# Causal attention beside a mixture of experts: heads divided by VectorE and projected by pairs, and the combine spread over more units

## The reference

```python
xn  = layernorm(x)                        # no gamma, no beta
# attention: 16 heads of 64, RMS norm with gamma, causal softmax
normed = xn / max(norm(xn), 1e-12) * 128 ** 0.5 * gamma
q, k, v = split(normed @ w_qkv)           # 128 x 3072
attn = softmax(where(causal, q @ k.T / 8, -max))
attention = (attn @ v, heads side by side) @ w_out      # 1024 x 128
# experts: top 2 of 8, 128 -> 512 -> 128, relu
experts = layernorm(xn + sum over the two of weight * expert(xn)) * ffn_gamma + ffn_beta
out = x + attention + experts
```

## Time and profile before

| | |
|---|---|
| median of 3 runs | 1457.95 us (1456.97 to 1460.27) |
| profiled execution, its own time | 1463.13 us |
| its span (first to last instruction) | 1461.4 us |
| mean granted TensorE clock | 0.958 |
| TensorE busy | 1351.4 us, 92% |
| VectorE busy | 1038.1 us, 71% |
| ScalarE busy | 947.8 us, 65% |
| GpSimd busy | 867.2 us, 59% |

### The profile page before, as it was taken

The page is one execution under the profiler, slowest core; times in us unless marked ns, Lnnn a source line. Parts: engine busy times, 40 slices in busy tenths (PEclk is TensorE's granted clock), DMA queues, the critical chain, the costliest instruction groups (busy, mean ns, idle before and its releaser), DMA issues.

```text
span 1461.4 us, 27770 instructions
## 1 busy us (share of the span) xinstructions
PE 1351.4 (92%) x8360; PEld 1124.9 (77%) x8361; DVE 1038.1 (71%) x2674; ACT 947.8 (65%) x2094; POOL 867.2 (59%) x1304
## 2 busy tenths in 40 slices
PE   4569998999879999999999899899899999899998
PEld 4446666999757888788788788788788788788886
DVE  5656654222257788888888888888888888888773
ACT  2435544555447677677777677677677777677775
POOL 3426651332227568667667667767766766766666
PEclk9669999999869999999999999999999999999999
DMA  6222221222122022112112212112212212211112
GB/s 204 89 60 63 63 54 55 77 75 77 47 57 52 3 41 50 29 30 51 35 33 44 43 30 46 38 36 42 41 30 46 42 32 39 48 30 32 30 30 59
DMA packets 131078, 72.47 MB, mean 50 GB/s; under 512 B 80216, under 2 KB 116864, under 8 KB 130944
## 3 DMA queue, kind: packets, MB, share of 16 engines
q1 hardware_dynamic: 114304, 54.18, 18.2%
q0 software_dynamic: 4096, 8.40, 1.9%
q10 hardware_dynamic: 12544, 8.29, 1.9%
HBM read 20.47 MB, written 16.52 MB: 25 GB/s over the span
## 4 chain that ended last, share of the span: by engine, by line
PE 53%; DVE 11%; issue 5%; ACT 2%; DMA 1%; SPq 0%; DVEq 0%; POOLq 0%; ACTq 0%
PE max_ps L1281 8%; PE score_ps L1299 6%; PE score_ps L1298 6%; PE misc_ps L1341 6%; PE head_ps L1318 5%; PE head_ps L1327 5%; PE head_ps L1325 5%; PE head_ps L1323 5%; DVE max_ps L1140 4%; PE misc_ps L1262 3%; DVE x_row L1156 2%; PE misc_ps L1256 2%; DVE q_a L1126 1%; PE misc_ps L1257 1%; PE misc_ps L1258 1%
## 5 line engine op out<-in xcount | busy, mean ns | idle before, releaser
L1032 POOL TENSOR_TENSOR p_lo<-probs,p_hi 128x512 fp32r<-128x512 f32 (+3 forms) x560 | 536.1, 958 | 188.5 <-ACT p_hi L1084 183.9
L1082 ACT ACTIVATE probs<-score_ps 128x512 f32<-128x512 f32 (+3 forms) x768 | 377.5, 492 | 257.0 <-PE score_ps L1299 243.8
L1140 DVE CUSTOM_DVE_ANT_0 max_ps<-max_ps,mask 128x128 f32<-128x128 f32 (+7 forms) x512 | 390.7, 763 | 111.1 <-PE max_ps L1281 87.8
L1298 PE MATMUL score_ps<-q_a,k_a 128*128 128x512 f32 (+3 forms) x768 | 304.3, 396 | 0.2 <-ACT p_hi L1084 0.2
L1281 PE MATMUL max_ps<-k_a,q_a 128*128 128x512 f32 (+3 forms) x768 | 238.6, 366 | 54.2 <-DVE shift L1140 45.0
L1024 POOL TENSOR_SCALAR_AFFINE_SELECT probs<-probs 128x128 f32<-128x128 f32 x512 | 153.7, 300 | 202.3 <-ACT p_hi L1084 136.9
L1299 PE MATMUL score_ps<-q_b,k_b 65*128 65x512 f32 (+3 forms) x768 | 269.6, 351 | 0.0
L1084 ACT ACTIVATE p_hi<-score_ps 128x512 fp32r<-128x512 f32 (+3 forms) x560 | 263.1, 470 | 0.0
L1318 PE MATMUL head_ps<-probs,v_all 128*65 128x128 f32 (+3 forms) x1088 | 248.7, 310 | 0.0
L1281 PEld LDWEIGHTS max_ps<-k_a,q_a 128*128 128x128 f32 x768 | 140.8, 195 | 114.9 <-DVE shift L1140 86.5
L1323 PE MATMUL head_ps<-p_hi,v_hi 128*65 128x512 f32 (+3 forms) x560 | 210.3, 376 | 0.0
(11 more groups left out here) (165 smaller groups left out, 2086.6 us busy)
## 6 DMA issues: line engine op xcount, KB each, us to landing
k_a<-k_a SPq DMA_DIRECT2D x64, 256.0 KB
q_b<-q_a SPq DMA_DIRECT2D x64, 256.0 KB
q_b<-shift SPq DMA_DIRECT2D x512, 0.5 KB
sorted_x<-zeros SPq DMA_DIRECT2D x13, 384.0 KB, 5.0
rows<-sorted_x SPq DMA_DIRECT2D x39, 128.0 KB, 2.1
sorted_y<-result ACTq DMA_DIRECT2D x39, 128.0 KB, 1.8
acc<-in_L_attn_x_dram SPq DMA_DIRECT2D x4, 512.0 KB, 7.2
x_row<-in_L_attn_x_dram SPq DMA_DIRECT2D x8, 256.0 KB
```

Source lines behind the costliest of these rows:

```text
L1032: pool.tensor_tensor(p_lo[:, lo_slot(g, c), w0:w1], probs[:, slot, w0:w1], p_hi[:, slot, w0:w1].bitcast(F32), ALU.subtract).then_inc(pool_ ...
L1082: ins = act.activation(probs[:, slot, 0:width], src[:, 0:width], ACT.Exp, scale=SCALE)
L1140: dve.tensor_tensor_reduce(out=max_ps[:, at:at + width], in0=max_ps[:, at:at + width], in1=mask[:, SEQ - width:SEQ], scale=-1.0, scalar=-M ...
L1298: pe.matmul(dst, k_a[i][s][:, keys], q_a[i][s][:, qs], start=True, stop=False)
```

## The change

- **Projection by pairs.** For all heads but the last two of each stage, ScalarE copies the head with its row of sums into raw. SP moves the 1024 sums out of their one partition into [128, 8] (sums, chunk 5 of the next unit), VectorE inverts them (chunk 8), SP writes them to a row in DRAM (inverse, chunk 10) and reads the row back into 64 partitions (spread, chunk 0 of the unit after). At chunks 3 and 4 of that unit VectorE multiplies the two halves of the head with it into stacked, rows 0 to 63 for the even head, 64 to 127 for the odd one. At chunks 7 and 9 of an odd unit TensorE projects both heads at once with 128 rows, in two pieces of four tiles, and VectorE adds each piece to acc in one instruction. The last two heads of each stage go the old way.
- **Combine.** 33 steps a group instead of 45, seven to a unit at chunks 0, 2, 4, 5, 7, 9 and 11, in units 3 to 7 of the group. Centring goes to ScalarE (chunks 7 to 10 of unit 2). The norm and gamma are one step, the scale and the addition to acc another; ffn_beta is added to acc by GpSimd, in 8 instructions at the start of the expert stage, before it waits for w1_split.
- **nT in DRAM.** nT is stored to DRAM in the routing stage in 8 DMAs, and ScalarE's queue loads 1024 tokens of it for each batch's projection of v (tokens). The new tiles take its room.
- **Start and end.** The pieces of q and k come in the order q, k, q, k, and SP copies each half by itself (eight DMAs of half the size). Only t0 to t3 of the first unit's maxima stand before its first score, t4 to t7 at its chunks 0 and 1, and those of the second unit from chunk 2. The last batch is stored in three DMAs, of 3, 3 and 2 tiles.

```diff
+                        pool.wait_ge(beta_loaded, 16)
+                        for g in range(ALL_TILES // GROUP):
+                            some = acc[:, g * GROUP:(g + 1) * GROUP]
+                            pool.tensor_tensor(some, some, fbeta[:].unsqueeze(1).broadcast_to([P, GROUP, D]),
+                                               ALU.add).then_inc(beta_added, 1)
...
+                    return own + [(W + 1, t) for t, at in enumerate(SECOND_MAX_AT) if at == c]
+                return [(W + 1, t) for t, at in enumerate(MAX_AT) if at == c and W + 1 < WL]
 
             PROJECT_AT = [{0: 0, 1: 1, 3: 2, 5: 3}, {1: 4, 5: 5}]
 
             STARTS = [6 * k for k in range(ALL_TILES // GROUP)]
             GATHER_AT = [(1, 8)] + [(1, c) for c in (9, 10, 11)] + [(2, c) for c in (1, 3, 5, 7, 9)]
             SCATTER_AT = [(g, c) for g in range(7) for c in range(10)][:2 * ALL_TILES]
-            COMBINE = ([("center", q) for q in range(GROUP)]
-                       + [("first", q) for q in range(GROUP)] + [("second", q) for q in range(GROUP)]
+            COMBINE = ([("first", q) for q in range(GROUP)] + [("second", q) for q in range(GROUP)]
                        + [("stats", q) for q in range(GROUP)] + [("aggr", 0), ("var", 0)]
                        + [("rsqrt", n) for n in range(RSQRT_STEPS)]
-                       + [(kind, q) for kind in ("norm", "gamma") for q in range(GROUP)]
-                       + [(kind, q) for q in range(GROUP) for kind in ("beta", "add")])
+                       + [(kind, q) for q in range(GROUP) for kind in ("gamma", "add")])
             COMBINE_STEPS = len(COMBINE)
-            COMBINE_AT = [(2, c) for c in (2, 4, 5, 6)]
-            COMBINE_AT += [(g, c) for g in (3, 5) for c in (0, 0, 1, 2, 3, 4, 5, 5, 6, 7, 8, 9, 11, 11)]
-            COMBINE_AT += [(7, c) for c in (0, 0, 1, 2, 3, 3, 3, 4, 4, 5, 5, 7, 7)]
+            COMBINE_AT = [(g, c) for g in (3, 4, 5, 6) for c in (0, 2, 4, 5, 7, 9, 11)]
+            COMBINE_AT += [(7, c) for c in (0, 2, 4, 5, 7)]
+            CENTRE_AT = [(2, c) for c in (7, 8, 9, 10)]
             assert len(COMBINE_AT) == COMBINE_STEPS
-            Y_AT = [7, 9, 11]
...
+            Y_AT = {7: 0, 9: 1}
+            LAST_Y_AT = {8: 0, 10: 1, 11: 2}
...
+                    if W % 2 and c in Y_AT and stacks(W - 2):
+                        order += [(kind, W // 2 - 1, Y_AT[c]) for kind in ("y", "add")]
+                    if W == WL - 1 and c in LAST_Y_AT:
+                        order += [(kind, W - 1, LAST_Y_AT[c]) for kind in ("last_y", "last_add")]
+                    if c:
+                        order += [("shift", *item) for item in max_items(W, c - 1)]
+                    if stacks(W - 1):
+                        order += [(kind, W - 1, 0) for kind, at in (("sums", 5), ("invert", 8), ("inverse", 10))
+                                  if at == c]
+                    if stacks(W - 2):
+                        order += [(kind, W - 2, n) for kind, n, at in (("spread", 0, 0), ("norm", 0, 3),
+                                                                      ("norm", 1, 4)) if at == c]
...
+                        if (unit - start, c) in CENTRE_AT:
+                            order.append(("centre", CENTRE_AT.index((unit - start, c)), k))
+                        order += [("combine", n, k) for n, at_ in enumerate(COMBINE_AT) if at_ == (unit - start, c)]
...
+                        if kind == "sums":
+
+                            W = g
+                            sp.wait_ge(heads_out[0], W + 2)
+                            sp.wait_ge(heads_out[1], W + 2)
+                            sp.dma_start(sums[:, W % 2], raw[HEAD:HEAD + 1, W % 2]).then_inc(sums_moved[W % 2], 16)
+                        if kind == "inverse":
+                            W = g
+                            sp.wait_ge(sums_inverted, n_stacked(W) + 1)
+                            sp.dma_start(inverse_row[W % 2].rearrange("(p j) -> p j", p=P), inverse[:, W % 2]
+                                         ).then_inc(inverse_moved[W % 2], 16)
+                        if kind == "spread":
+                            W = g
+                            sp.wait_ge(inverse_moved[W % 2], n_spread(W) * 16)
+                            if native and W == W0:
+                                for q in range(BATCH):
+                                    sp.wait_ge(nT_stored[q], 16 * SEQ // BANK)
+                            if W > W0:
+                                sp.wait_ge(norm_done, 2 * n_stacked(W - 1) + 2)
+                            sp.dma_start(rden_all[:], inverse_row[W % 2].partition_broadcast(HEAD)
+                                         ).then_inc(spread[W % 2], 16)
...
+                    def load_tokens(Q):
+                        cols = slice(Q % BATCH * SEQ, (Q % BATCH + 1) * SEQ)
+                        if Q > Q0:
+                            act.wait_ge(misc_ready, place[("project", Q - 1, 5)] + 1)
+                        if Q < BATCH:
+                            act.wait_ge(nT_stored[Q], 16 * SEQ // BANK)
+                        act.dma_start(tokens[:], nT_dram[:, cols]).then_inc(tokens_loaded, 16)
...
+                        elif kind == "centre":
+                            row, t = x_row[:, g], c * GROUP + g
+                            act.wait_ge(x_again, c * 16 + 16)
+                            act.activation(row, row, ACT.Identity, scale=rstd[:, t:t + 1],
+                                           bias=centre_bias[:, t:t + 1]).then_inc(centred, 1)
...
+                            if half == 0 and W - W0 >= 2:
+                                act.wait_ge(norm_done, 2 * n_stacked(W - 2) + 2)
...
-                        elif kind == "norm":
-                            ins = dve.tensor_scalar(row, row, gmom[:, n, 0:1], gvar[:, 1, n:n + 1],
-                                                    ALU.subtract, ALU.mult)
                         elif kind == "gamma":
-                            ins = dve.tensor_tensor(row, row, fgamma[:], ALU.mult)
-                        elif kind == "beta":
-                            ins = dve.tensor_tensor(row, row, fbeta[:], ALU.add)
+                            if step == COMBINE.index(("gamma", 0)):
+                                dve.wait_ge(small2_loaded, 16)
+                            ins = dve.scalar_tensor_tensor(out=row, in0=row, scalar=gmom[:, n, 0:1], in1=fgamma[:],
+                                                           op0=ALU.subtract, op1=ALU.mult)
                         elif kind == "add":
-                            ins = dve.tensor_tensor(acc[:, t], acc[:, t], row, ALU.add)
+                            ins = dve.scalar_tensor_tensor(out=acc[:, t], in0=row, scalar=gvar[:, 1, n:n + 1],
+                                                           in1=acc[:, t], op0=ALU.mult, op1=ALU.add)
                         ins.then_inc(comb_step, 1)
...
+                    def invert(W):
+                        dve.wait_ge(sums_moved[W % 2], n_spread(W) * 16)
+                        if W - W0 >= 2:
+                            dve.wait_ge(inverse_moved[W % 2], n_spread(W - 2) * 16)
+                        dve.reciprocal(inverse[:, W % 2], sums[:, W % 2]).then_inc(sums_inverted, 1)
+
+                    def normalise(W, half):
+
+                        s, cols = W % 2, slice(half * BANK, (half + 1) * BANK)
+                        rows = slice(s * HEAD, (s + 1) * HEAD)
+                        if half == 0:
+                            dve.wait_ge(spread[s], n_spread(W) * 16)
+                            if s == 0 and W // 2 > Q0:
+                                dve.wait_ge(misc_ready, place[("y", W // 2 - 1, 1)] + 1)
+                        dve.tensor_tensor(stacked[rows, cols], raw[0:HEAD, s, cols], rden_all[:, cols],
+                                          ALU.mult).then_inc(norm_done, 1)
+
+                    def after_combine(n):
+                        if n:
+                            dve.wait_ge(comb_step, n)
+
+                    def add_y(Q, n):
+                        u = place[("y", Q, n)]
+                        rows = acc[:, Q % BATCH * TILES + n * GROUP:Q % BATCH * TILES + (n + 1) * GROUP]
+                        dve.wait_ge(misc_ready, u + 1)
+                        dve.tensor_tensor(rows, misc_ps[u % 2][:].rearrange("p (t d) -> p t d", d=D), rows,
+                                          ALU.add).then_inc(y_added, 1)
+
...
+                    def project_pair(Q, n):
+                        dst = misc_bank("y", Q, n)
+                        pe.wait_ge(norm_done, 2 * n_stacked(2 * Q + 1) + n + 1)
+                        if n == 0:
+                            pe.wait_ge(wout_loaded, Q // BATCH * 16 + 16)
+                        for q in range(GROUP):
+                            q0 = (n * GROUP + q) * P
+                            ins = pe.matmul(dst[:, q * D:(q + 1) * D], stacked[:, q0:q0 + P], wo[:],
```

(3 more changed lines are left out.)

652 lines of the change are left out of this document (329 added, 323 removed).

## The result

The changed kernel takes 1490.16 us (median of 5 runs, 1486.9 to 1490.5), beside 1459.35 of the kernel before on the same chip: ratio 1.0206, 95% interval 1.019 to 1.0222. A first series of 4 runs gave 1490.71 and 1.0217 (1.0165 to 1.0269). The forecast was 1440, faster; the range reached to 1480. The direction was wrong, and the time lies outside the range.

What follows compares the result with a forecast made beforehand. TensorE was taken to bound a pair, with some 7.4 us a combine period lost to waits. Terms -14 - 3 - 4 - 2.5 + 7.5 - 2 = -18, and 5.2 for the profiled run, gave 1440 us; range 1415 to 1457, eight in ten 1385 to 1480.

Steps and rivals of the forecast that it cites:

- Inverse sums, "Hidden": Three more DMAs a unit on SP's queue (sums, inverse, spread): claimed hidden, with 1 us in hand.
- The two attention stages, -14 and -3: Second stage: eight combine periods, each 1.7 us shorter, -14 us; first stage: -3, between 0 and -5.4.
- 110.4, the figure that was forecast: Second attention stage: a combine period of three pairs was to take 110.4 us, from 112.1.
- The wait of 2 to 3 us in front of t6: Even units: TensorE waits 2 to 3 us before the sixth maximum; under 0.5 would mean the second case holds.
- The chain in front of the sixth maximum: VectorE before t5 in even units: normalisations 2.0 and combine steps 1.2 come in, 0.8 waiting absorbs part; t5 2.4 later.
- the even unit's projection: Chunks 7, 9, 11: 16 of a pair's 32 records go, all the even unit's, 1.79 us off.
- Normalisation, 2.0 for two: VectorE, even unit, chunks 3 and 4: 0.69 each plus 0.6 held behind GpSimd, 2.0 us; ends 1.4 and 4.0.
- Starts, -4 and -2.5: Copies by halves remove TensorE's 3.79 us wait: -4 at the second attention start, between 0 and -9; -2.5 at the first.
- Experts, +7.5 (5 to 10): Expert stage start: GpSimd's eight beta additions delay the first w_now to 261.5; +6, with the clock +7.5 us.
- End, -2: Kernel end: the last store is 128 KB instead of 512, -2 us.
- TensorE's saving whole: Rival: VectorE fits and the projection's saving comes whole, 1362 us; half or whole saving (below 1415) had chance 0.25.
- The slow rival: Normalisation held behind GpSimd in every even unit, clock falling in each: +54, 1494 us; slower (above 1457) chance 0.28.

Runs made afterwards that it cites:

- tokens_odd: Changed kernel with each pair's token load moved from chunk 7 of the even unit to chunk 7 of the odd unit before; ratio 1.0014 to the kernel before.
- all_moved: Changed kernel with sums sent by ScalarE, whole first head first, beta beside expert blocks, combine in odd units, second normalisation in chunk 7, tokens in odd unit; 1405.24 us, 0.9628.
- start_shifts: Changed kernel, starts still by halves, but SP issues the next batch's first-half copies behind the shifts of the first head's last four tiles; ratio 1.0099.
- start_whole: Changed kernel with all eight maxima of the first head and their shifts in front of the first score in both attention stages; ratio 1.0065.
- beta_beside: Changed kernel with GpSimd's eight beta additions moved behind the weight copies of the first and last expert blocks; ratio 1.0127.
- three: Changed kernel with sums sent by ScalarE, the whole first head in front of the first score, and beta additions beside the expert blocks; ratio 0.9876.
- three_combine: Kernel with sums by ScalarE, whole first head first and beta beside expert blocks, plus combine steps in odd units only, from chunk 2 of unit 3; ratio 0.9675.
- late_invert: Changed kernel with reciprocal moved from chunk 8 to 10, inverse store to 11, spread to chunk 1, normalisations to chunks 4 and 5; 1577.12 us, ratio 1.0807.

## Why the prediction was wrong

*Inverse sums, "Hidden": the step that failed.* The text names the danger itself, sums behind the copies, asked for in chunk 8, and then reckons only with the spread. The spread was in time in the changed kernel, but for 2 waits of 9.2 us; the sums were late 28 times, for 70.3 us of VectorE's time. Of the 32 token loads of 512 KB that the diff brings, the prediction weighs one, at the first start; the others are at nothing, without a reason. Their moment is worth 28 us.

*The two attention stages, -14 and -3.* With nothing but the tokens moved, the profile of tokens_odd has 1004.8 for the second stage and 126.8 for the first: -14.6 and -5.2 against the kernel before. Its eight periods average 110.4, the figure that was forecast, and the pair without combine takes 34.70, as good as unchanged. Some of this agreement may be luck: each is one execution, before's lay 5.2 us above the median of its runs and this one 3.6 below, so that up to 9 us of the difference may be theirs. The chain in front of the sixth maximum, the combine and the projection were thus weighed about right together; that each single term was is not shown. The wait of 2 to 3 us in front of t6, by which the prediction wanted to be judged, is not there in the changed kernel (1.66 at most); in tokens_odd it is 31.6 us in 25 times between 460 and 1380 us, 2.23 at most. For the even unit's projection the nearest figure is the pair without combine, 1.0 us shorter in all_moved than before, of the 1.79 of its records.

*Normalisation, 2.0 for two.* 831 ns each, 1.66 for two, less than I took. The 39 of 120 during which no p_lo subtraction of GpSimd ran took 0.69 in the mean, the 77 with one beside them 0.90.

*Starts, -4 and -2.5.* Wrong in sign. The copies by halves did remove the wait of 3.79, but I did not cost what each shift stands behind in SP's queue. start_shifts has the size: 15.6 us for that order in both starts, and start_whole 20.6 for the whole division.

*Experts, +7.5 (5 to 10).* The mechanism was right; 11.5 by beta_beside. The copy of weights came at 269.06 where I had 261.5, since the stage as a whole began some 8 us later; without the additions it comes at 259.41.

*End, -2.* -0.6 in the profiled execution.

*The rivals.* "TensorE's saving whole", 1362, is not reached even by all_moved. Its premise was right in part: matmuls added in the odd unit count nearly in full, and the even unit's saving shows once the waits are gone. The slow rival's 1494 lies near the result by coincidence: its mechanism, normalisations held in full and a clock that falls in each even unit, isn't there. The normalisations took 0.83 us in the mean, and the clock is below 0.97 in 10 of the stage's 27 pairs, against 6 before. three at 1440.35 matches the forecast for no better reason.

The account of the changed kernel, in single edits, is 28 us for the tokens' moment (19 of them also to be had by sending the sums from ScalarE), 21 for the starts and 11.5 for beta: 60 us, if they add, which in this combination was not run. tokens_odd, three, three_combine and all_moved compute the whole, so these are losses of placing and not of the idea: with the placing changed the same idea takes 3.7% off the kernel before.

## What to carry to other kernels

Cost every transfer that a change adds, and for each small one that an engine waits for ask two things: what is issued ahead of it in its own queue, and which large transfer is in flight on the other queues at that moment. A load with a unit's time to spare should be put where no short, awaited transfer follows it. Moving a step later is no safe way to hide it: it can be moved behind something dearer, as late_invert shows.

## What was not expected of the hardware

A 4 KB transfer on SP's queue took 3.8 us behind 512 KB on ScalarE's queue, against a median of 2.1, and moving the large one gave 1.9% of the kernel's time. Gathered rows behind a 256 KB transfer showed the same, 3 us against at most 1.7. SP takes about 0.64 us to issue each 128 KB copy between partitions, so that four of them are 2.5 us of queue. In the second start that was the smaller part of what the shifts stood behind: SP waited for the copies' own data until 440.73, when the first of these shifts had been ready for 9 us.
